# Two-layer kernel on one core: another order of the loads and of the split passes in the first three groups

## The reference

```python
attn_in = tanh(einsum('bsd,da->bsa', x, W1) + b1)          # A = 128
scores = einsum('bsa,a->bs', attn_in, v)
# mask by type 0, 1, 2: l <= j, l >= j, l != j
p = softmax(where(mask, scores[:, None, :], -1e30), axis=-1)
x = x + einsum('bjl,bld->bjd', p, x) / cnt[..., None]
out = x + einsum('bsd,bdh->bsh', x, W[cat]) + b[cat][:, None, :]
```

## Time and profile before

| | |
|---|---|
| median of three executions | 321.86 us (321.63 to 322.38) |
| the profiled execution | 322.09 us |
| its span, first to last instruction | 320.3 us |
| TensorE, VectorE, ScalarE busy | 97%, 89%, 86% |
| granted clock of TensorE | 0.994 |
| moved by DMA | 101.5 MB, 316 GB/s over the span |

### The profile page before, as it was taken

How to read it: one execution, slowest core, us unless ns; L and a number is a source line. 1 busy time by engine, 2 the same in 40 slices (tenths; PEclk the granted TensorE clock), 3 DMA queues, 4 the chain that set the end, 5 groups by cost and what they waited for, 6 DMA issues and landing times.

```text
span 320.3 us, 4751 instructions
## 1 busy us (share of the span) xinstructions
PE 311.7 (97%) x1374; PEld 242.3 (76%) x1374; DVE 283.8 (89%) x300; ACT 274.4 (86%) x447; POOL 3.6 (1%) x17
## 2 busy tenths in 40 slices
PE   8999897999999999999999999999999999999996
PEld 4445675878888887887888788888878888787884
DVE  3558799999999999999999999999999999999950
ACT  2376988979989899998989999898998989899852
POOL 3010000000000000000000000000000000000000
PEclk9999997999999999999999999999999999999999
DMA  7999999899989989998999999898899989974123
GB/s 227 429 356 422 421 382 335 303 354 308 356 308 345 353 300 381 303 376 299 358 322 320 351 328 368 313 350 317 307 405 297 360 311 353 334 282 178 37 96 131
DMA packets 21290, 101.49 MB, mean 317 GB/s; under 512 B 2385, under 2 KB 2386, under 8 KB 11282
## 3 DMA queue, kind: packets, MB, share of 16 engines
q1 hardware_dynamic: 20882, 100.15, 85.2%
q10 hardware_dynamic: 288, 0.79, 0.7%
q0 software_dynamic: 96, 0.26, 0.3%
HBM read 84.41 MB, written 16.78 MB: 316 GB/s over the span
## 4 chain that ended last, share of the span: by engine, by line
PE 91%; ACT 3%; DVE 2%; DMA 2%; issue 1%; SPq 0%; DVEq 0%; ACTq 0%
PE ps_y L564 17%; PE ps_y L565 16%; PE ps_y L566 16%; PE ps_pre L520 11%; PE ps_y L579 4%; PE ps_y L552 4%; PE ps_y L576 4%; PE ps_y L577 4%; PE ps_y L578 4%; PE ps_pre L509 2%; PE ps_pT L543 2%; DMA x_raw<-in_x 2%; PE ps_scores L530 1%; DVE w_lo L378 1%; PE ps_scores L532 1%; ACT w_hi L261 1%
## 5 line engine op out<-in xcount | busy, mean ns | idle before, releaser
L378 DVE TENSOR_TENSOR w_lo<-w_raw,w_hi 128x2048 fp32r<-128x2048 f32 x60 | 137.1, 2285 | 4.0 <-ACT w_hi L261 4.0
L261 ACT ACTIVATE w_hi<-w_raw 128x2048 fp32r<-128x2048 f32 x60 | 115.9, 1933 | 1.5 <-DVE w_raw L366 1.5
L564 PE MATMUL ps_y<-w_hi,xT_hi 128*128 128x512 f32 x240 | 96.6, 403 | 0.3 <-DVE w_lo L378 0.3
L566 PE MATMUL ps_y<-w_hi,xT_lo 128*128 128x512 f32 x240 | 94.4, 394 | 0.0
L565 PE MATMUL ps_y<-w_lo,xT_hi 128*128 128x512 f32 x240 | 94.4, 393 | 0.0
L566 PEld LDWEIGHTS ps_y<-w_hi,xT_lo 128*128 128x128 f32 x240 | 45.3, 189 | 10.0
L564 PEld LDWEIGHTS ps_y<-w_hi,xT_hi 128*128 128x128 f32 x240 | 45.4, 189 | 9.6 <-ACT out_sb L303 0.5
L565 PEld LDWEIGHTS ps_y<-w_lo,xT_hi 128*128 128x128 f32 x240 | 45.4, 189 | 9.3
L405 DVE TENSOR_TENSOR z_lo<-ps_y,z_hi 128x512 fp32r<-128x512 f32 x64 | 43.5, 682 | 6.3 <-ACT z_hi L297 6.3
L297 ACT ACTIVATE z_hi<-ps_y 128x512 fp32r<-128x512 f32 x64 | 39.0, 610 | 9.3 <-PE ps_y L566 4.8
L366 DVE TENSOR_TENSOR w_raw<-w_raw,ident 128x512 f32<-128x512 f32 x63 | 42.8, 681 | 0.6 <-DMA w_raw<-in_L_cond_W 0.6
(11 more groups left out here) (71 smaller groups left out, 284.5 us busy)
## 6 DMA issues: line engine op xcount, KB each, us to landing
w_raw<-in_L_cond_W SPq DMA_DIRECT2D x63, 1024.0 KB, 8.3
out<-out_sb SPq DMA_DIRECT2D x64, 256.0 KB, 5.4
x_raw<-in_x SPq DMA_DIRECT2D x15, 1024.0 KB, 7.1
w_raw<-in_L_cond_W SPq DMA_DIRECT2D x2, 512.0 KB, 6.6
x_raw<-in_x ACTq DMA_DIRECT2D x1, 512.0 KB, 5.9
x_raw<-in_x SPq DMA_DIRECT2D x1, 512.0 KB, 5.2
w_pack<-in_W_b_v ACTq DMA_DIRECT2D x1, 257.0 KB, 3.2
b_raw<-in_L_cond_b POOLq DMA_DIRECT2D x2, 128.0 KB, 7.2
```

The lines of the kernel that those rows point to most:

```text
L261: nc.scalar.activation(w_hi[k % NH][:], w_raw[k % NW][:], ACT.Copy).then_inc(w_hi_ready, 1)
L378: nc.vector.tensor_tensor(w_lo[k % NL][:], w_raw[k % NW][:], w_hi[k % NH][:].bitcast(F32), ALU.subtract).then_inc(w_lo_ready, 1)
L564: nc.tensor.matmul(y[:], xT_hi[q][:, c, xs], w_hi[k % NH][:, c, :], start=(c == 0), stop=False)
L566: last = nc.tensor.matmul(y[:], xT_lo[q][:, c, xs], w_hi[k % NH][:, c, :], start=False, stop=(c == DC - 1))
```

## The change

The code of TensorE keeps its order. What is changed:

- SP loads both halves of x0, waits for the second half, and then issues W1, W2, x1, W4, W3, W5, the bias, x2, W6. W0 is one load from ScalarE's queue.
- Because W4 arrives ahead of W3, its identity addition and its splits come ahead of W3's, and `wi_count` gives 5 for sample 4 and 6 for sample 3.
- row_div moves from VectorE to GpSimd, for all 16 groups; the reciprocal stays on VectorE.
- On ScalarE and VectorE the lists for samples up to 8 have a new order, and reach further: the splits of x of group 2 and of W5 to W9 stand earlier.
- In the loop of ScalarE, `split_w_hi(k + 3)` goes ahead of `exp_group` at the last sample of each group.
- The ids are spread over the partitions by a bf16 product instead of a float32 one, and one of the 20 warm-up products is left out.

```diff
         def wi_count(k):
-            return k + 2
+            return {3: 6, 4: 5}.get(k, k + 2)
...
             sp.dma_start(ids_row[:], ids.rearrange("(a n) -> a n", a=1)).then_inc(ids_in, 16)
-            sp.dma_start(x_raw[0][:, halves[0], :], xg[0][:, halves[0], :]).then_inc(x0_in[0], 16)
+            for h, c in enumerate(halves):
+                sp.dma_start(x_raw[0][:, c, :], xg[0][:, c, :]).then_inc(x0_in[h], 16)
             sp.wait_ge(ids_in, 16)
-            cat_0 = sp.value_load(ids_row[0:1, 0:1], min_val=0, max_val=C - 1)
-            for h, c in enumerate(halves):
-                sp.dma_start(w_raw[0][:, c, :], w[bass.ds(cat_0, 1), :, c, :].rearrange("a p c h -> p (a c) h"))\
-                    .then_inc(w0_in[h], 16)
+            sp.wait_ge(x0_in[1], 16)
             load_w(1)
             load_w(2)
             load_x(1)
+            load_w(4)
             load_w(3)
-            load_w(4)
             load_w(5)
+            sp.dma_start(b_raw[0:C, :], bias).then_inc(b_low_in, 16)
+            sp.dma_start(b_raw[C:P, :], bias).then_inc(b_high_in, 16)
             load_x(2)
             load_w(6)
...
-            pool.wait_ge(w_in[2], 16)
-            pool.dma_start(b_raw[0:C, :], bias).then_inc(b_low_in, 16)
-            pool.dma_start(b_raw[C:P, :], bias).then_inc(b_high_in, 16)
+            pool.wait_ge(seen_ready, 1)
+            for g in range(GROUPS):
+                pool.wait_ge(exp_ready, g + 1)
+                if g >= 1:
+                    pool.wait_ge(scale_ready, g)
+                nc.gpsimd.tensor_tensor(row_div[:], row_sum[:], seen[:, G * g:G * (g + 1)], ALU.mult)\
+                    .then_inc(div_ready, 1)
...
-            act.dma_start(x_raw[0][:, halves[1], :], xg[0][:, halves[1], :]).then_inc(x0_in[1], 16)
             act.wait_ge(warm_ready, 1)
             nc.scalar.activation(table[:], warm[:, 0:1], ACT.Tanh)
+            act.wait_ge(ids_in, 16)
+            cat_0 = act.value_load(ids_row[0:1, 0:1], min_val=0, max_val=C - 1)
+            act.dma_start(w_raw[0][:], w[bass.ds(cat_0, 1)].rearrange("a p c h -> p (a c) h")).then_inc(w_in[0], 16)
...
                 if b == 2 and g + 1 < GROUPS:
                     tanh_group(g + 1)
+                if b == 3 and k + 3 < B:
+                    split_w_hi(k + 3)
                 if b == 3 and g + 1 < GROUPS:
                     exp_group(g + 1)
                 copy_out(k - 3)
                 if b == 0 and g + 1 < GROUPS:
                     split_xT_hi(g + 1)
-                if k + 3 < B:
+                if b != 3 and k + 3 < B:
                     split_w_hi(k + 3)
...
             def row_scale_group(g):
-                dve.wait_ge(exp_ready, g + 1)
-                nc.vector.tensor_tensor(row_div[:], row_sum[:], seen[:, G * g:G * (g + 1)], ALU.mult)\
-                    .then_inc(div_ready, 1)
                 dve.wait_ge(div_ready, g + 1)
                 nc.vector.reciprocal(row_scale[:], row_div[:]).then_inc(scale_ready, 1)
```

More of the change, by code:

```diff
@@ L117, in program @@
         x0_in = [sem(f"x0_in{h}") for h in range(2)]
-        w0_in = [sem(f"w0_in{h}") for h in range(2)]
         x_in = [sem(f"x_in{i}") for i in range(NX)]
@@ L321, in _ @@
             nc.scalar.activation(b_both[:], b_raw[:], ACT.Copy).then_inc(b_hi_ready, 1)
-            tanh_group(1)
-            split_w_hi(4)
+            split_w_hi(5)
+            split_xT_hi(2)
+            exp_group(1)
             split_z_hi(3)
-            split_w_hi(5)
-            exp_group(1)
             copy_out(0)
             scale_group(1)
+            split_w_hi(6)
+            split_mix_hi(1)
+            split_z_hi(4)
             copy_out(1)
-            split_xT_hi(2)
-            split_w_hi(6)
+            copy_out(2)
             split_w_hi(7)
-            for k in range(G + 1, B + 3):
+            split_z_hi(5)
+            split_w_hi(8)
+            tanh_group(2)
+            copy_out(3)
+            split_w_hi(9)
+            for k in range(G + 3, B + 3):
                 g, b = k // G, k % G
@@ L444, in _ @@
                                            ALU.is_equal, ALU.add).then_inc(bias_ready, 1)
+            dve.wait_ge(w1_hi_ready, 1)
+            nc.vector.tensor_tensor(w1_lo[:], w1_raw, w1_hi[:].bitcast(F32), ALU.subtract)\
+                .then_inc(w1_lo_ready, 1)
+            add_identity_0(0)
+            add_identity_0(1)
+            split_av_lo(0)
             add_identity(1)
@@ L447, in _ @@
             add_identity(2)
-            dve.wait_ge(seen_ready, 1)
+            split_z_lo(0)
             row_scale_group(0)
-            split_z_lo(0)
-            split_z_lo(1)
+            add_identity(4)
             split_xT_lo(1)
             add_identity(3)
+            split_w_lo(4)
+            add_identity(5)
+            split_z_lo(1)
             split_mix_lo(0)
-            add_identity(4)
+            split_av_lo(1)
             dve.wait_ge(b_hi_ready, 1)
@@ L475, in _ @@
             add_identity(9)
-            for k in range(G + 2, B + 1):
+            split_av_lo(2)
+            split_z_lo(5)
+            split_w_lo(8)
+            add_identity(10)
+            for k in range(G + 3, B + 1):
                 g, b = k // G, k % G
@@ L587, in _ @@
             warm_up(9)
-            pe.wait_ge(ones_ready, 1)
-            pe.wait_ge(ids_f_ready, 1)
-            nc.tensor.matmul(ps_pT[:, 0:2 * B], ones[0:1, :].bitcast(F32), ids_f[:], start=True, stop=True)\
+            pe.wait_ge(ones_ready, 2)
+            pe.wait_ge(ids_bf_ready, 1)
+            nc.tensor.matmul(ps_pT[:, 0:2 * B], ones_bf[:], ids_bf[:], start=True, stop=True)\
                 .then_inc(ids_spread, 1)
-            warm_up(11)
+            warm_up(10)
             hidden_raw(0)
```

41 lines of the change are left out of this document (18 added, 23 removed).

## The result

| | before | changed |
|---|---|---|
| median of four executions each, same chip | 322.05 us (321.63 to 322.38) | 318.83 us (318.54 to 319.18) |
| the profiled execution | 322.09 us | 318.58 us |
| its span | 320.3 us | 316.2 us |
| what lies outside the span | 1.8 us | 2.4 us |

A forecast was written before the change was run, and what follows sets the result against it. TensorE, busy 311.7 of 320.3 us, was taken as the bound, with 6.4 us lost before group 2's transposes. -6.4 + 0.5 + 0.25 + 0.8 + 0.2 = -4.65 us from the 321.86 median gave 317.2 us, range 315.3 to 319.4.

The forecast's parts named there:

- w_hi ahead of exp: Loop, last sample of each group: exp starts at most 0.6 us later within 2.1 us of slack, so 0.
- stalls and slow clock before T(2): Before group 2's transposes: four TensorE stalls and the 0.88 granted clock go, -6.4 us.
- pz(0) later (W0's head and the bias): First residual product of sample 0: W0 landing whole costs +0.5 us, waiting for the bias split +0.25.
- what is late next: T(2), hidden(3), scores(3): Group 2's transposes 0.1 us, hidden(3) 0.5 and scores(3) 0.2 late: +0.8 us, bounds 0 and 3.
- row_div: Moved to GpSimd, it may wait for VectorE's running operation: +0.2 us, bounds 0 and 2.2.
- a remainder: 3.95 us of idle TensorE in 28.9 to 51.8, listed with the slow clock beside the four stalls.
- the 24.25 worked out for a full engine: First residual product to group 2's transposes: one group period (18.67 us) plus 24 large products (5.6 us).
- the walk: The forecast's stepping of three engines through their new order, with row durations and loads landing 2.49 us per MB.
- The rival in which the head costs nothing: Prologue: W0 lands at 9.4, W1 by 13; +0.5 and +0.25 vanish: 316.0 us or a little under, chance 0.14.
- a sign of being wrong: Around group 2: w_hi(8) or w_hi(10) waits over 1.5 us for its identity addition, or the reciprocal waits for GpSimd.
- the first rival: Group 2's chain has no slack, so the stall moves further: 1.3 to 2.2 us more, 318.5 to 319.4, chance 0.20.
- The rival in which this edit makes the kernel slower: Scaled probabilities late in all 14 loop groups; at 0.5 us a group it costs 7: 324.2 us, chance 0.07.

The follow-up runs named there:

- the second session: The changed kernel again, with no edit, in another session: median 317.64 us, ratio 0.9857 to the kernel before.

## Why the prediction was right, and by how much its steps were off

Forecast was 317.2 us, with 315.3 to 319.4 around it; measured 318.83, and 317.64 in the second session. The mechanism held and the terms were off in both directions. That the time came inside the range is in part luck: without the 0.8 us from w_hi ahead of exp, for which the sum had nothing, the median would be 319.6, outside it. By the windows shown above:

| term | predicted | profiled execution | second session |
|---|---|---|---|
| stalls and slow clock before T(2) | -6.4 | -6.4 | -6.4 |
| pz(0) later (W0's head and the bias) | +0.75 | +1.7 | +0.9 |
| what is late next: T(2), hidden(3), scores(3) | +0.8 | +1.4 | +1.3 |
| row_div | +0.2 | with the one above | with the one above |
| w_hi ahead of exp in the loop | 0 | -0.8 | -0.8 |
| outside the span | 0 | +0.6 | +0.5 |

*The stalls.* Right; the first row of the table is by definition what is left when the third is counted apart. Waits at T(1), xw(5) and scores(2) are gone and the granted clock is 1.00. (The 3.95 us of idle TensorE that the prediction calls a remainder are those stalls seen once more, 4.75 by the distances; the rest is mostly the slow clock. T(2) was forecast at 54.7 and came at 55.98, and at 55.06 in the second session.) From pz(0) to T(2) 24.76 us pass, 0.5 above the 24.25 worked out for a full engine.

*W1 and the head.* xw_raw(0) at 10.45 (10.7 forecast) and W1's identity addition at 13.35 (14.1). W1 was issued at 8.38 (8.5) and took 4.95 to land, where I had taken 5.6 as the quickest load; it was not, the quickest W load of the same trace took 5.1. From W2 to W3 the landings were 0.2 to 0.3 behind the walk. The rival in which the head costs nothing did not come either: xw_raw(0) is 0.45 later than the 10.00 of before.

*The bias on SP's queue was mis-sized.* I took its bytes, 0.6, and nothing above them. Between W3's landing and x2's lie W5, the bias and x2, 24.3 to 31.1: 6.8 us, where two loads at 2.49 and 0.6 for the bias give 5.6. It costs 1.2 above its bytes (0.9 in the second session, 23.91 to 30.35), nearly as much as the 1.4 from GpSimd. The same reading gives 0.7 to 1.8 over the seven runs that load it there without a dry queue, so one execution does not fix this price. W5 landed at 27.8 instead of 26.6, and the bias at 28.8 instead of 27.2.

*pz(0).* My walk said that pz(0) would wait for the bias split. It waits for av_lo(1): scores(1) needs that, and pz(0) starts 0.77 behind it. With av_lo(1) ending at 29.7, as walked, both ways give 30.45, so the number was right through the wrong wait, and in the second session, where av_lo(1) ends at 29.6, pz(0) does start at 30.45. In the profiled execution av_lo(1) ends at 30.39: 0.25 of it is W4's later landing, 0.28 the wait for W5, the rest single handoffs on VectorE. (Measured against the timeline's 29.52 instead of the chain's 29.71, pz(0) is later by another 0.2, which is why the table has 1.7.)

*What is late next.* hidden(3) waits where the walk had it (0.5 forecast; its start at 60.73 follows 0.57 behind its due time). At T(2) the walk had 0.1; the two windows hold 0.5 ahead of T(2) and 0.88 behind it. w_hi(10) waited 1.45 for its identity addition, just under the 1.5 that I had named as a sign of being wrong. It is the first rival, in a third of its least size, 0.4 us above the 1.0 of my two terms where the rival had 1.3 or more: VectorE is full to 0.1 us from T(2) to T(3). The median does lie in that rival's interval, 318.5 to 319.4, but pz(0) and the time outside the span carried it there.

*row_div.* It took 0.20 us alone, and 0.41, 0.69 and 0.64 in groups 0 to 2 beside an identity addition, with which it ends: the addition at 34.55 runs to 35.24, row_div from 34.60 to 35.29, and the reciprocal starts at 35.32. Without row_div in between the reciprocal would come at 35.15, so it costs 0.17 here, just under the 0.2 to 0.4 of my walk. The reciprocal does wait for GpSimd, which I had named as a sign of being wrong; in group 2 the same 0.17 is a part of what T(2) waits. The rule that the prediction cited (the Trainium skill, SBUF — State Buffer, section "SBUF: two separate sides") agrees with these durations. In the kernel with exp ahead of w_hi the median over 16 groups is 0.64, against 0.20 in the changed kernel, since there row_div meets a running w_lo.

*w_hi ahead of exp.* The direction was wrong. I asked what the later exp would delay, found 2.1 us of slack, and took 0. I did not ask what the earlier w_hi would release. The wait list of TensorE after 60 us was empty although these waits were there; they add up to 0.8 us over 12 groups. The rival in which this edit makes the kernel slower had the sign wrong as well.

*Outside the span.* I took it as a constant. It is 1.73 to 1.79 in kernels with the old loads and row_div on VectorE (before, and three others), 1.96 with row_div on GpSimd, 2.05 to 2.12 with the new loads (also with the bias put back to GpSimd), and 2.34 to 2.4 with both. So about 0.2 to 0.3 goes with row_div on GpSimd and 0.3 to 0.4 with the new loads. Why an instruction on GpSimd or a load on another queue adds time there isn't settled.
